# First Wg in the SM tiles, batch 1's first chunk pairs loaded during batch 0, and the weight splits moved out of S of batch 1

## The reference

```python
# x, ctx: (8, 512, 2048) = (batch, channel, position), float32
def xattn(q, k, v):                      # q = layernorm(x), k = v = ctx
    t, p, g = Wt @ v, Wp @ q, Wg @ k     # (512 x 512) @ (512 x 2048), each batch
    att = sum(p * g) over each of 8 groups of 64 channels and all positions
    y = blockdiag(Wz) @ (att * t)        # 64 x 64 blocks
    return groupnorm(y) * gn_w + gn_b + v
x = x + xattn(layernorm(x), ctx, ctx)
h = layernorm(x)[:, :, perm]             # positions permuted, 16 heads of 128
h = gelu(h_head @ up[head]) @ down[head] # (128 -> 512 -> 128), exact gelu
x = x + unpermuted h
```

## Time and profile before

| | before |
|---|---|
| median of three runs | 1608.36 us (1607.37 to 1610.45) |
| the profiled execution | 1607.69 us, of it 1605.9 us from first to last instruction (the span) |
| TensorE busy | 1518.3 us, 95%, 6592 matmuls |
| VectorE, ScalarE, GpSimd busy | 80%, 61%, 54% |
| mean granted TensorE clock | 0.99 |
| DMA | 233 GB/s mean over the span |

### The profile page before, as it was taken

One profiled execution on the slowest core, in us unless ns is written; L12 is line 12 of the kernel. 1 busy time (PEld: TensorE's weight loads), 2 busy tenths in 40 slices (PEclk: granted clock), 3 DMA queues, 4 the chain that ended last, 5 costly groups with the idle time before them and its releaser, 6 DMA issues.

```text
span 1605.9 us, 19290 instructions
## 1 busy us (share of the span) xinstructions
PE 1518.3 (95%) x6592; PEld 1234.1 (77%) x6592; DVE 1279.0 (80%) x1736; ACT 974.7 (61%) x1061; POOL 874.1 (54%) x765
## 2 busy tenths in 40 slices
PE   8998899999989999999999999899998999986997
PEld 6776677877878887788877888688886888765885
DVE  5878979696996879879797888968789697866664
ACT  4334538734776367763677537774487735985785
POOL 1284437157871268613784238832388125976784
PEclk9999999999999999999999999999999999998999
DMA  8788968686776747677386755848568584569685
GB/s 320 288 291 317 331 203 307 247 286 214 239 277 191 251 127 256 248 222 232 118 283 216 249 189 174 283 172 257 163 201 297 156 260 155 190 163 286 207 291 179
DMA packets 126288, 374.77 MB, mean 233 GB/s; under 512 B 24560, under 2 KB 32752, under 8 KB 118000
## 3 DMA queue, kind: packets, MB, share of 16 engines
q1 hardware_dynamic: 91888, 251.88, 47.3%
q0 software_dynamic: 34304, 121.66, 22.4%
HBM read 287.45 MB, written 86.03 MB: 233 GB/s over the span
## 4 chain that ended last, share of the span: by engine, by line
PE 45%; POOL 17%; DVE 17%; DMA 10%; issue 7%; ACT 3%; SPq 0%; POOLq 0%; DVEq 0%; ACTq 0%
PE PP L835 14%; PE PP L849 13%; PE PP L903 7%; PE PP L888 6%; POOL FB L1255 5%; PE PP L862 5%; POOL FB L1252 4%; POOL out L1260 4%; DMA FB<-xg_scratch,perm_sb 3%; DVE R L1017 3%; POOL FB L1240 2%; DVE X L1029 2%; DMA WW<-w_scratch 2%; DVE R L1169 2%; DVE Z L1134 2%
## 5 line engine op out<-in xcount | busy, mean ns | idle before, releaser
L888 PE MATMUL PP<-GG,WW 128*128 128x512 f32 x1536 | 394.2, 393 | 38.8 <-DVE GG L1164 23.4
L835 PE MATMUL PP<-R 128*128 128x512 f32 x1536 | 360.7, 394 | 18.0 <-DVE R L1017 16.2
L888 PEld LDWEIGHTS PP<-GG,WW 128*128 128x128 f32 x1536 | 286.8, 189 | 111.5 <-issue 50.4
L849 PE MATMUL PP<-R,WC 128*128 128x512 f32 x1536 | 352.8, 391 | 7.6 <-ACT Z L934 4.1
L835 PEld LDWEIGHTS PP<-R 128*128 128x128 f32 x1536 | 290.9, 190 | 83.1 <-issue 18.5
L849 PEld LDWEIGHTS PP<-R,WC 128*128 128x128 f32 x1536 | 288.9, 188 | 70.4 <-ACT Z L934 6.8
L903 PE MATMUL PP<-R,WW 128*128 128x512 f32 x1050 | 271.1, 394 | 12.4 <-DMA WW<-w_scratch 6.0
L981 ACT ACTIVATE PP<-PP 128x1024 f32<-128x1024 f32 x256 | 261.6, 1022 | 0.0
L1169 DVE TENSOR_TENSOR R<-PP,R 128x1024 fp32r<-128x1024 f32 x175 | 213.1, 1218 | 60.4 <-ACT PP L981 60.3
L980 ACT ACTIVATE R<-PP 128x1024 fp32r<-128x1024 f32 x175 | 179.7, 1027 | 125.5 <-PE PP L888 125.3
L903 PEld LDWEIGHTS PP<-R,WW 128*128 128x128 f32 x1050 | 195.6, 189 | 58.4 <-issue 17.3
(11 more groups left out here) (91 smaller groups left out, 1639.4 us busy)
## 6 DMA issues: line engine op xcount, KB each, us to landing
WW<-w_scratch SPq DMA_DIRECT2D x152, 512.0 KB, 5.6
X<-in_x SPq DMA_DIRECT2D x32, 1024.0 KB, 5.5
RAW<-in_cx SPq DMA_DIRECT2D x32, 1024.0 KB, 9.2
RAW<-in_xT SPq DMA_DIRECT2D x63, 512.0 KB, 6.3
RAW<-in_cT SPq DMA_DIRECT2D x63, 512.0 KB, 8.6
xg_scratch<-FB POOLq DMA_DIRECT2D x104, 256.0 KB, 6.2
w_scratch<-WW POOLq DMA_DIRECT2D x16, 1024.0 KB, 5.7
RAW<-in_Wg SPq DMA_DIRECT2D x8, 1024.0 KB, 8.3
```

What stands on the lines that cost most here:

```text
L835: t = eng.matmul(s_bank(c1), l[:, part(c1)], r, start=(dt == 0 and j == 0), stop=(dt == ND - 1 and j == 2))
L849: t = eng.matmul(PP[2 + ot // 2][:, ot % 2, :], WC[:, l, ct, part(ot)], u[:, r + ct, :], start=(ct == 0 and j == 0), stop=(ct == NT - 1 an ...
L888: t = eng.matmul(PP[slot["up", f, p]][:, e, :], wt[:, l, part(2 * p + e)], g[:, r, :], start=(j == 0), stop=(j == 2))
```

## The change

Batch 0's Wg goes to the SMM tile (the two SM tiles together), which nobody uses before batch 0's transposes, and no longer takes a place in the ring of RAW tiles. The first three chunk pairs of batch 1 are put at base - 15, - 11 and - 8 in place of - 5, - 3 and + 0.3. Slot zero splits heads 10 to 15, 0 and 1 instead of 8 to 15; S of batch 1 splits none; y of batch 1 splits heads 2, 3, 8 and 9 from two RAW tiles, as y of batch 2 goes on doing with 4 to 7, and heads 8 and 9 stay in WW for the FFN that follows, so that their four `load_w` fall away. Batch 1's Wg takes the tile of its last ctx quarter and moves from y0 + 3.5 to y0 + 9. `s_fix`, `s_evh` and `s_evl` of batches 0 and 1 are put 0.6 later.

```diff
+YHEADS = {1: (2, 3, 8, 9), 2: (4, 5, 6, 7)}
...
     def load_wg(i):
-        k = slot["wg", i] = slot["c", i, 3] if i == 2 else ring("raw", NRAW)
-        free["wg", i] = take(("raw", k))
-        n.dma("wg", i, sem=f"raw{k}")
+        if i == 0:
+            n.dma("wg", 0, sem="wg0")
+        else:
+            k = slot["wg", i] = slot["c", i, 3] if i < 3 else ring("raw", NRAW)
+            free["wg", i] = take(("raw", k))
+            n.dma("wg", i, sem=f"raw{k}")
...
-            give(t, ("raw", slot["wg", i]))
+            give(t, *([("raw", slot["wg", i])] if i else [("SM", 0), ("SM", 1)]))
...
     def raw_w(h):
-        if 4 <= h < 8:
-            return [("raw", slot["c", 2, 1 + h // 2 % 2])]
-        k = 2 * (h % 2) if h > 7 else 4
+        for i in (1, 2):
+            if h in YHEADS[i]:
+                return [("raw", slot["c", i, 1 + YHEADS[i].index(h) // 2])]
+        k = 2 * (h % 2)
         return [("FB", k), ("FB", k + 1)]
...
     for k in range(8):
         t = 15 + 2.6 * k
-        put(t, load_raw, 8 + k)
-        put(t + 4, w_hi, 8 + k)
-        put(t + 4.1, w_lo, 8 + k)
-        put(t + 4.2, keep_w, 8 + k)
-    for h in range(4):
-        t = 38 + 4 * h
-        put(t, load_raw, h)
-        put(t + 2.6, w_hi, h)
-        put(t + 2.7, w_lo, h)
-        put(t + 2.8, keep_w, h)
+        put(t, load_raw, (10 + k) % ND)
+        put(t + 4, w_hi, (10 + k) % ND)
+        put(t + 4.1, w_lo, (10 + k) % ND)
+        put(t + 4.2, keep_w, (10 + k) % ND)
...
-        for k, h in enumerate((4, 5, 6, 7) if i == 2 else ()):
-            put(y0 + (2.5, 5.2)[k // 2], load_raw, h)
-            put(y0 + 5.6 + 1.8 * k, w_hi, h)
-            put(y0 + 5.7 + 1.8 * k, w_lo, h)
-            put(y0 + 5.8 + 1.8 * k, keep_w, h)
+        late = 1.0 if i == 1 else 0
+        for k in range(4 if i == 1 or i == 2 else 0):
+            h = YHEADS[i][k]
+            put(y0 + (2.5, 5.2)[k // 2] + late, load_raw, h)
+            put(y0 + 5.6 + 2 * late + 1.8 * k, w_hi, h)
+            put(y0 + 5.7 + 2 * late + 1.8 * k, w_lo, h)
+            put(y0 + 5.8 + 2 * late + 1.8 * k, keep_w, h)
         for j in range(8):
-            put(s0 + (S_LOAD[j] if i > 1 else 0.3 if (i, j) == (1, 2) else 2 * j - (5 if i or j else 10)), load_s, i, j)
+            put(s0 + (S_LOAD[j] if i > 1 else (-15, -11, -8)[j] if i and j < 3 else 2 * j - (5 if i or j else 10)), load_s, i, j)
...
-        put(y0 + (9 if i == 2 else 2.5 + late), load_wg, i)
+        put(y0 + (9 if 0 < i < 3 else 2.5), load_wg, i)
...
         for c1 in range(NT):
-            put(y0 + 11.3 + 0.6 * c1, s_fix, i, c1)
-            put(y0 + 11.5 + 0.6 * c1, s_evh, i, c1)
-            put(y0 + 12.2 + 0.6 * c1, s_evl, i, c1)
+            put(y0 + 11.3 + (0.6 if i < 2 else 0) + 0.6 * c1, s_fix, i, c1)
+            put(y0 + 11.5 + (0.6 if i < 2 else 0) + 0.6 * c1, s_evh, i, c1)
+            put(y0 + 12.2 + (0.6 if i < 2 else 0) + 0.6 * c1, s_evl, i, c1)
...
-                if x < 2 and i == 2:
+                if x < 2 and i < 3:
                     kept.append((w + x, j, h))
                     continue
...
+    def wg_tile(i):
+        return RAW[slot["wg", i]] if i else SMM
...
             elif stage == "load_wg":
+                if a[0] == 0:
+                    eng.dma_start(SMM[:], Wg.rearrange("(t p) o -> p t o", p=P)).then_inc(S["wg0"], 16)
+                    continue
```

More of the change, by code:

```diff
@@ L390, in raw_w @@
     def raw_w(h):
-        if 4 <= h < 8:
-            return [("raw", slot["c", 2, 1 + h // 2 % 2])]
-        k = 2 * (h % 2) if h > 7 else 4
+        for i in (1, 2):
+            if h in YHEADS[i]:
+                return [("raw", slot["c", i, 1 + YHEADS[i].index(h) // 2])]
+        k = 2 * (h % 2)
         return [("FB", k), ("FB", k + 1)]
     def load_raw(h):
-        sem = f"rh{h}" if 4 <= h < 8 else f"rw{h % 2 if h > 7 else 2}"
+        sem = f"rh{h}" if h in YHEADS[1] + YHEADS[2] else f"rw{h % 2}"
         free["rw", h] = take(*raw_w(h))
@@ L592, in plan @@
         put(y0 + 2.1, root_x, i)
-        late = 1.0 if i == 1 else 0
         for q, t in enumerate((s0 + 9, s0 + 11, s0 + 13, y0 + 1.5 + late)):
             put(t, load_c, i, q)
-        put(y0 + (9 if i == 2 else 2.5 + late), load_wg, i)
+        put(y0 + (9 if 0 < i < 3 else 2.5), load_wg, i)
         for q, t in enumerate((y0 - 3, y0 + 0.4, y0 + 4.3, y0 + 8.3)):
@@ L1078, in vector @@
                         dve.wait_ge(*t)
-                eng.tensor_tensor_reduce(out=s_bank(ot), in0=s_bank(ot), in1=RAW[slot["wg", i]][:, ot, :], scale=1.0,
+                eng.tensor_tensor_reduce(out=s_bank(ot), in0=s_bank(ot), in1=wg_tile(i)[:, ot, :], scale=1.0,
                                          scalar=0.0, op0=ALU.mult, op1=ALU.add,
```

## The result

The kernel after takes 1606.3 us (median of 16 runs, 1600.95 to 1613.97) against 1612.01 us for the kernel before beside it on the same chip (16 runs, 1603.62 to 1616.46): ratio 0.9966, 95% interval [0.9951, 0.9981]. It is faster, by 5.5 us where 11 were forecast. Run twice more, unaltered, it gave 0.9958 [0.9941, 0.9976] and 0.9953 [0.9937, 0.9969]. The kernel before had medians of 1610 to 1613 us in five of the six sets of runs made beside it, and 1616 in one, so the 1608.36 us of the first three runs lay at its low end. Both the time and the forecast of it hang on that, the ratio doesn't.

The account below looks back on a forecast made before the run. TensorE sets the time, so only its idle time or low-clock matmuls can yield gains: 1.0 + 13.0 - 2.9 = 11.1 us off 1607.69 gives 1596.6, with the median 0.7 above, so 1597 us; range 1590 to 1602.5.

Parts of the forecast that it names:

- the prediction's fourth: y of batch 1 with four splits: +3.8 stalls gone, -1.4 Wp wait, -5.3 late gather; sum -2.9 us, bounds -6.5 and +2.4.
- Wg into SMM, early pairs: Loads of batch 0's Wg and batch 1's chunk pairs: one pair at about 69, three before 93; 0 us by itself.
- the prediction's "why" of S: S of batch 1, 58.9 us for 43.5 of matmuls: late chunk pair first, then GpSimd's splits stretching VectorE's additions.
- `s_fix` later, 1.0: y of batch 0: its 2.18 us stall moves to V's start as 2.2 us; gain 1.0 us, bounds 0.2 and 4.
- S of batch 1, 13.0: S of batch 1 without its splits and one chunk pair takes 46 us; gain 13.0 us, bounds 10 and 14.2.
- middle 4.2 plus 1.1 for the clock: TensorE's idle time before batch 1's first `up_mm`, 1.8 to 7.8 us, middle 4.2; clock 1.1 (1.8, six times in ten).
- T + 54 if a tile waits 2.64 us: First gather's issue, T being y of batch 1's start: T + 51.3, or T + 54 if a tile waits for a store.
- The rest, 0: Batch 1's Wg at y0 + 9, renumbered heads, two `load_w` dropped, remaining program: 0, with 1 us either way.
- B: Rival: S of batch 1 stays slow, only half its loss goes; 5 us gained, 1602.5 us; chance 0.15.
- D: Rival: nothing reaches the end, gains in S eaten by y; within 3 us of before, 1607 us; chance 0.04.
- C: Rival: y's splits wait for stores, gather near T + 61, loss 12 us; with 20 us lost, 1611 us; chance 0.04.
- A: Rival: GpSimd's queue is early enough, the first gather of batch 1 lands in V; 18 us gained, 1590 us; chance 0.17.

Follow-up runs that it names:

- e6: The kernel after without the early pairs, Wg of batch 0 in the ring again, the splits still moved: 1608.42 us, ratio 0.9979.
- e5: The kernel before with only Wg of batch 0 in SMM and the early chunk pairs, splits left in S: 1607.5 us, ratio 0.9973.
- e3: The kernel before with only `s_fix`, `s_evh` and `s_evl` of batches 0 and 1 put 0.6 later: 1611.64 us, ratio 1.001.
- e2: The kernel after with head 9's split behind the first two gathers in batch 1: 1603.93 us, ratio 0.9949.
- e9: The kernel after with head 7's split in batch 2 behind the first three gathers: 1603.09 us, ratio 0.9935.
- f1: The kernel after, batch 1's y splits storing a sixteenth and computing the low part for an eighth of columns, wrong results: 1594.18 us, ratio 0.9852.
- f2: The kernel after with batch 1's splits ordered as in e1 and batch 2's as in e9: 1601.61 us, ratio 0.9910.
- f3: The kernel after with batch 1's splits ordered as in e2 and batch 2's as in e9: 1602.24 us, ratio 0.9907.
- e1: The kernel after with the splits of heads 2 and 8 one place earlier in GpSimd's queue in batch 1: 1601.22 us, ratio 0.9937.
- f4: f2 run again, unaltered, beside the kernel after: 1601.36 us, ratio 0.9920 to the kernel before.

## Why the prediction had the direction right and the size wrong

The kernel became faster, but by half of what was forecast, and 1606.3 us lies outside of 1590 to 1602.5. The step that failed is the prediction's fourth, the idle time ahead of the first `up_mm` with its clock: 5.3 us in the sum, 9.4 us in the traces. By its own steps:

1. *Wg into SMM, early pairs.* The order came as told: Wg ahead, a pair early, three out before 93. SyncE of the kernel after, Wg and the two pairs' first loads:

```profile
62.64 0.50 SPq L1323 DMA_DIRECT2D SMM<-in_Wg  x1
67.69 0.34 SPq L1300 DMA_DIRECT2D RAW<-in_xT  x1
...
88.38 0.33 SPq L1300 DMA_DIRECT2D RAW<-in_xT  x1
...
89.84 0.33 SPq L1300 DMA_DIRECT2D RAW<-in_xT  x1
```

But the prediction's "why" of S was half wrong. It put the late pair first and the splits second; e6 shows that the pairs are worth 0.4 us of S where the splits have left (45.8 and 45.4). Where they have not, e5's 54.5 lies among the 52.3, 58.9 and 60.5 of the two profiles of before and e3. Whether they are worth anything in the whole, the ratios of e6 and the kernel after don't tell; their intervals overlap.

2. *`s_fix` later, 1.0.* The stall moved to V as forecast (2.32, 1.99 and 2.19 us in the three profiles). The lower clock followed it in one of them, 0.86 over V, which took 12.6 us; V took 11.0 in the other two. The prediction counted the lower clock behind two of three such idle times; it left out a fourth, 2.32 us ahead of 161.92 in S of batch 1, after which 24 matmuls took 7.33 us, so it was three of four. S of batch 1 starts at a mean of 114.7 instead of 116.4, 1.7 earlier; e3 gives nothing for this part alone. Right within what can be told.

3. *S of batch 1, 13.0.* 45.4 us three times against a forecast of 46; 47.9 to 48.2 us in e2, e9, f1 and f2, which have the same S, where `v_att` kept TensorE waiting 1.9 to 2.3 us in place of 1.1 and the lower clock followed. The stage was right. The gain of S and y together, the wait for Wp included, was forecast at 15.4 us (13.0 + 3.8 - 1.4) and came to 15.3 to 19.2, from 106.2 and 109.0 to 89.8 to 90.9.

4. *y of batch 1, -2.9.* Here the prediction failed. y itself is without a stall, and V waits 1.54, 1.79 and 0.73 us for Wp, about the 1.4 forecast. The estimate of 4.4 us that the prediction set beside this wait is from a fit of the Trainium skill ("DMA: Bandwidth & Descriptors", on the anatomy of one DMA) for DMAs issued by GpSimd; this load is SyncE's, and took 12.0, 12.3 and 11.2 us to land. The term that was mis-sized is "middle 4.2 plus 1.1 for the clock". Idle before the first `up_mm` are 7.48, 6.59 and 8.14 us, and the low clock costs 2.0 (4 us at 0.50): 9.4 us in the mean instead of 5.3. The sum had both bounds at hand: the first gather at T + 51.3 or "T + 54 if a tile waits 2.64 us", and it came at T + 54.3; and from gather to a running `up_mm` 4.9 or 6.9 us, and it took 6.8 (213.60 to 220.41). I took a middle, as though these terms did not hang together. The sum's own upper end, 7.8 us idle and 1.8 for the clock, is 9.6, and that is what came: the store of head 2 took 10.6 us in a full stretch, and the gather behind it 5.19 us to land instead of 3.6. The 16.3 MB that I gave y are 11.6 (45.2 us at 257 GB/s); V and the FFN have 18.0 (66.8 us at 270) where they had 14.2 (56.2 us at 252), so part of the traffic arrived where the gathers are. The small gaps in the FFN, each for a `load_w`, are no part of the miss: 0.69, 1.37 and 0.91 us after, and 0.65, 0.81 and 1.59 before, the last of them here:

```profile
270.08 1.63 PE L903 MATMUL PP<-R,WW 128*128 128x512 f32 x6 [1.59 <-DMA WW<-w_scratch]
```

V and FFN together took 56.1 us before and 67.2 after (means), 11.1 lost where 5.3 were forecast. In sum from S of batch 1 to the end of its FFN: 163.7 us before (mean of two), 157.7 after (mean of three), 6.0 gained of 10.1 forecast.

5. *The rest, 0.* From S of batch 2 to the end of its FFN the two profiles of before took 197.6 and 200.3 us, the three of after 202.8, 200.3 and 203.5; that is 3 us lost in the mean. e9 and f3 show that the stall at the start of the FFN can be had back by head 7's place in GpSimd's queue, which is the same stall as in batch 1. But the kernel before has it too, 1.63 us in its first profile and as much as in the kernel after in its second:

```profile
384.33 2.43 PE L888 MATMUL PP<-GG,WW 128*128 128x512 f32 x6 [3.22 <-DVE GG L1164]
```

Whether the kernel after really loses here is open: V and FFN of batch 2 took 104.5 to 108.0 us in the four profiles with the plan of before (both of before, e3, e5) and 106.8 to 111.4 in the ten that end batch 2 as the kernel after does. The means differ by 2.4 us, the ranges overlap, and no run shows a cause.

Of the rivals, B gives the size (half of the gain) for a reason that did not occur: S is quick. D, gains in S eaten by y, describes what became of two thirds of the gain of S and y (17.1 us gained in the mean, 11.1 lost behind them), but the rest did reach the end. C named the right mechanism, stores that hold WW tiles and so the gather, on the wrong scale; its 2.83 us wait is the first stage of it, and T + 54 lies far from its T + 63. A was wrong: the queue of GpSimd is not early enough until both the traffic and the passes are gone (f1).

## What to carry to other kernels

Work moved from one crowded stretch to another is priced at the second by the worst of the rows that depend on the same traffic, all together and not by the middle of each: late store, late gather and low clock came at once. If removing one suspect leaves the stall, look what the next instruction waits for and remove both; a stall with two limits close together gives back little to either alone. If a stall shrinks, look whether what it waited for is earlier, or only the stage that it stood in later (e1). Before one stage's time is taken as the kernel's, profile the kernel twice: here one stage moved by 9 us between two profiles while its sum with the neighbour moved by 3.

## What was not expected of the hardware

A store of 1 MB from GpSimd's queue landed 10.6 us after its issue in the second half of y, against a median of 5.6 us for the twelve from 60 to 240 us. The low half of Wp, loaded by SyncE, took 11.7 us in the kernel before, 11.2 to 12.3 in the three profiles of after, and 16.1 in e1, where the store of head 2 had gone out 5 us ahead of it (186.99 against 192.14); in f2 and f4, with the same order, 16.7 and 15.8.

An instruction of VectorE with two operands in SBUF that met one of GpSimd's splits ended 1.08 us after it, seven times of seven in the kernel before; in the mean over S of batch 1, `s_lo` took 1606 ns in place of e6's 1267, and `x1_piece` 1808 in place of 1277.

After the idle time of 7.48 us the granted clock was 0.50 for 4 us, the lower level (1.2 GHz), with TensorE busy for 3.99 of them; after 6.59 and 8.14 us it was 0.50 as well. The short idle time at the start of V of batch 0 went either way: in 13 profiles it was 1.8 to 2.4 us, and V then took 11.0 us in nine of them and 12.6 in four; in the three where it was 3.2 to 3.4 us, V took 12.6 to 13.7.
